# Value steps placed two units earlier, with the ones and the rows of maxima behind them, and a shorter pause in the preparation

## What is computed

```python
x = x + xcond(_layernorm(x), ctx, ctx, itok)     # attention, per batch
#   heads of 32 rows; attn = softmax(SCALE * log(itok) * q^T k) over 512 keys
#   out[d, q] = sum over k of attn[q, k] * v[d, k]
x = x + ffn(_layernorm(x), ...)
#   8 experts, top 2 of 8, capacity int(T * 1.25 / 8); gelu(x w1 + b1) w2 + b2 + gelu(x wd) wu
#   and 0.2 times a shared expert of the same form on every token
```

## Time and profile before

| | |
|---|---|
| runs | 1389.69 us (1389.59 to 1391.52) |
| profiled execution, span | 1389.7 us |
| TensorE busy | 1344.6 us (97%) |
| VectorE busy | 815.9 us (59%) |
| ScalarE busy | 686.5 us (49%) |
| GpSimd busy | 250.6 us (18%) |
| shares of the chain that ended last | PE 84%, DVE 6%, ACT 5%, issue 3% |

### The profile page before, as it was taken

The page is one execution under the profiler, slowest core; times in us unless marked ns, Lnnn a source line. Parts: engine busy times, 40 slices in busy tenths (PEclk is TensorE's granted clock), DMA queues, the critical chain, the costliest instruction groups (busy, mean ns, idle before and its releaser), DMA issues.

```text
span 1389.7 us, 27089 instructions
## 1 busy us (share of the span) xinstructions
PE 1344.6 (97%) x11195; PEld 965.9 (70%) x11213; DVE 815.9 (59%) x1337; ACT 686.5 (49%) x1024; POOL 250.6 (18%) x219
## 2 busy tenths in 40 slices
PE   5788999999999999999999999999999999999997
PEld 2152736464555646484888889998888888888895
DVE  7776768696887877763734626446264362552620
ACT  4766666757575766663423425334253342442421
POOL 4630010010010041523102204022030030300202
PEclk9799999999999999999999999999999999999999
DMA  9513131313123232408545566555564565544403
GB/s 276 182 53 107 47 99 39 107 46 99 47 84 71 69 69 92 122 17 192 167 116 152 129 131 181 131 153 135 131 166 121 133 181 127 153 119 104 98 4 39
DMA packets 136747, 155.89 MB, mean 112 GB/s; under 512 B 59065, under 2 KB 79689, under 8 KB 136626
## 3 DMA queue, kind: packets, MB, share of 16 engines
q1 hardware_dynamic: 124338, 128.97, 32.2%
q0 software_dynamic: 12288, 25.21, 10.3%
HBM read 109.47 MB, written 34.15 MB: 103 GB/s over the span
## 4 chain that ended last, share of the span: by engine, by line
PE 84%; DVE 6%; ACT 5%; issue 3%; POOL 1%; DMA 0%; POOLq 0%; ACTq 0%; DVEq 0%
PE banks L1781 25%; PE banks L1811 24%; PE banks L1697 10%; PE banks L1715 9%; PE banks L1637 3%; PE banks L1617 3%; PE banks L1585 3%; DVE rowmax L1249 2%; ACT hidden L1038 2%; DVE late_stage L1270 1%; PE banks L1833 1%; ACT QS L1025 1%; PE banks L1646 1%; PE banks L1671 1%; PE banks L1822 1%
## 5 line engine op out<-in xcount | busy, mean ns | idle before, releaser
L1811 PE MATMUL banks<-hidden,w2h 128*128 128x0 bf16 x2048 | 313.0, 273 | 0.0
L1038 ACT ACTIVATE hidden<-banks,scales 128x512 f32<-128x512 f32 x256 | 170.1, 686 | 105.7 <-PE banks L1617 82.5
L1811 PEld LDWEIGHTS banks<-hidden,w2h 128*128 128x128 bf16 x2048 | 198.5, 98 | 25.6
L1811 PE MATMUL banks<-hidden,w2l 128*128 128x0 bf16 x1024 | 195.6, 273 | 0.0
L1249 DVE TENSOR_REDUCE rowmax<-banks 128x1 f32<-128x512 f32 x256 | 172.4, 684 | 36.8 <-PE banks L1585 34.7
L1132 ACT ACTIVATE hf<-banks,b1cols 128x640 f32<-128x640 f32 x128 | 101.5, 793 | 178.9 <-PE banks L1781 173.6
L1400 DVE TENSOR_TENSOR w1l<-stage,w1h 128x2048 bf16<-128x2048 f32 x32 | 73.2, 2291 | 198.8 <-ACT w1h L1115 198.8
L1715 PE MATMUL banks<-w2h,hidden 128*128 128x512 bf16 x512 | 184.4, 379 | 0.0
L1139 ACT ACTIVATE yT<-banks 128x640 f32<-128x640 f32 (+1 forms) x32 | 22.1, 690 | 270.1 <-PE banks L1811 270.1
L1781 PE MATMUL banks<-eth,w1h 128*128 128x0 bf16 x1024 | 136.0, 276 | 0.0
L1781 PE MATMUL banks<-eth,w1l 128*128 128x0 bf16 x1024 | 135.9, 276 | 0.0
(11 more groups left out here) (193 smaller groups left out, 1971.6 us busy)
## 6 DMA issues: line engine op xcount, KB each, us to landing
stage<-in_L_ffn_w SPq DMA_DIRECT2D x64, 1024.0 KB
split_parts<-hidden SPq DMA_DIRECT2D x16, 512.0 KB, 5.6
QS<-split_parts SPq DMA_DIRECT2D x48, 128.0 KB, 2.6
KS<-split_parts SPq DMA_DIRECT2D x48, 128.0 KB, 3.1
xin<-in_x SPq DMA_DIRECT2D x16, 256.0 KB, 3.6
cin<-in_ctx SPq DMA_DIRECT2D x16, 256.0 KB, 3.2
out_rows<-xin SPq DMA_DIRECT2D x16, 256.0 KB, 2.0
normed_rows<-x2r SPq DMA_DIRECT2D x16, 256.0 KB, 2.7
```

What stands on the lines that cost most here:

```text
L1038: ac.activation(prob[n % NPH], bank(score_bank[unit]), ACT.Exp, scale=scales[:, g // 2:g // 2 + 1]).then_inc(s_exp, 1)
L1811: issued = mm(half_of(bank(b0 + j)).shape_from_register(bank_cols(e, j)), w[:, fb, rows], half_of(a[:, fb, :], j).shape_from_register(slot ...
```

## The change

Three things, all in the plan. In the exponentials the value steps 0 to 2 of a group stand in the middle of iterations 5, 9 and 13, before the side streams and `down`, instead of at the end of 6, 10 and 14. The last value step of the even group stands in iteration 3 of the odd one with the ones directly behind it; in the up pass both stand behind the third turn. The rows of maxima of the odd group start at iteration 13 instead of 12 (windows 1 to 7), right behind value step 2. And `prepare` pauses two turns instead of four behind `rstd` in windows 1 to 6, for the side stream that runs beside the even group's exponentials.

```diff
-    def prepare(g):
-        for name, gaps in (("stats", 1), ("aggr", 1), ("rstd", 4), ("norm", 1), ("x_hi", 2), ("x_lo", 1), ("c_lo", 1), ("bounce", 1)):
+    def prepare(g, pause=4):
+        for name, gaps in (("stats", 1), ("aggr", 1), ("rstd", pause), ("norm", 1), ("x_hi", 2), ("x_lo", 1), ("c_lo", 1), ("bounce", 1)):
...
-                    side.append(prepare(g + 3 if w else g + 2))
+                    side.append(prepare(g + 3, 2) if w else prepare(g + 2))
...
+                if i % GH == 1 and i > GH:
+                    value_step(g, i // GH - 1)
+                if k == 1 and i == ONES:
+                    value_step(g - 1, QT - 1)
+                    if g - 1 in SUMMED:
+                        add("ones", g - 1)
                 if k == 0:
                     if i == (LATE + 2 if w else UNITS - 3):
                         add("parts", g + 1)
-                    elif i > (LATE + 3 if w else UNITS - 3):
+                    elif i > (LATE + 4 if w else UNITS - 3):
                         next(rows, None)
...
                 one_of(downs, 2 if k == 0 and i < 2 else 1)
-                if i % GH == 2 and (i > GH or k == 1):
-                    value_step(*divmod(g * QT + i // GH - 1, QT))
-                if k == 1 and i == ONES and g - 1 in SUMMED:
-                    add("ones", g - 1)
...
-            if n == 1:
+            if n == ONES - 1:
                 value_step(b, QT - 1)
-            if n == ONES - 1 and b in SUMMED:
-                add("ones", b)
+                if b in SUMMED:
+                    add("ones", b)
```

## The result

The changed kernel takes 1398.71 us (median of five, 1395.02 to 1400.47) against 1389.69 us before (1388.26 to 1391.52): ratio 1.0056, 95% interval 1.0039 to 1.0074. It is slower by 9.0 us where 6.0 were forecast. The profiled execution has a span of 1398.7 us and a time of 1400.47 us, the highest of its five: a time is 1.8 us more than the span of the same execution. The span of the kernel before, 1389.7, likewise belongs to the highest of its runs (1391.52), so the two traces differ by 9.0 as the medians do.

What follows compares the result with a forecast made beforehand. TensorE bounds the kernel, busy 73.16 of a steady window's 73.79 us. 1389.7 + 8.5 (windows 1 to 7) - 2.5 (window 0) = 1395.7 us; forecast 1392.5 to 1399.5, 8-in-10 range 1387 to 1401.5.

Steps and rivals of the forecast that it cites:

- Joins, 3.1 us for the ones: On TensorE, all 13 blocks of ones move directly behind a value step, each join saving 0.24 us.
- the 1.1 for window 1: Window 1 was to be 1.1 us longer: unit 2 late by 1.6, partly taken back by an idle stretch.
- Rows join, 1.4 us: On TensorE, rows of maxima joined to a value step save 0.20 us in each of 7 odd groups.
- VectorE's list 1.1 late behind step 0: Step 0 ahead of score 12 makes VectorE's list, its sum and ScalarE's exponential 10 come 1.1 us later.
- The pause, "moved, and not for nothing": On ScalarE, copies of x and context now precede exponential 11, so TensorE's unit 13 stalls about 0.5 us.
- `y` late, four copies, unit 2 late by 1.6: ScalarE's y 1.0 us later, then four row copies instead of three; odd group's unit 2 1.6 late, window 1.1 longer.
- Windows 5 and 6, 1.6 each: Small routing operations in VectorE's list make each of these windows lose 1.6 us.
- Window 7, 0.9: Without copies or normalization, but with four routing operations a unit, window 7 loses 0.9 us.
- Window 0, gain 2.5, between 0 and 4: In window 0, step 2 moves into TensorE's idle time before the rows of maxima, gaining 2.5 us.
- the joins winning: Rival: ScalarE and VectorE have more slack or the copies fit; 1382.7 us, down to 1378.5; chance 0.15.
- the cancellation: Rival: loss per window half the forecast's, y in time, unit 13 not waiting; 1390.7 us; chance 0.18.
- The clock did not fall in windows 2 to 7: Rival: stalls drop the clock to 1.2 GHz there, some 1.5 us each; 1404.7 us; chance 0.12.

Runs made afterwards that it cites:

- x4: Kernel before the change with only the last value step and the ones joined: 1388.83 us (one run), steady window 73.30 us against 73.79.
- x7: x6 with the pause cut from four turns to two: 1385.15 us (one run), steady window 73.28 us.
- x8: x7 with the parts of the normalised rows and the rows of maxima one iteration earlier in windows 1 to 6: 1385.14 us (five runs), ratio 0.9964.
- x2: Changed kernel with the rows of maxima back at iteration 12, not joined to value step 2: 1391.38 us (one run), steady window 74.06 us.
- x11: x6 with value step 2 alone one score earlier in windows 1 to 7: 1389.36 us (one run), steady window 73.80 us.
- x12: x6 with the rows of maxima one unit later in windows 1 to 7: 1385.42 us (one run), steady window 73.80 us.
- x9: x6 with value step 0 alone one score earlier in windows 1 to 7: 1390.61 us (one run), steady window 73.57 us.
- x3: Changed kernel with value step 0 of the even groups back behind unit 6 in windows 1 to 7: 1390.15 us (one run), steady window 74.37 us.
- x10: x6 with value step 1 alone one score earlier in windows 1 to 7: 1382.70 us (one run), steady window 73.32 us.
- x1: Changed kernel with the old pause of four turns: 1388.83 us (one run), steady window 74.43 us.
- x6: x4 with value steps 0 to 2 early in window 0 alone: 1384.80 us (five runs), ratio 0.9963 to the kernel before.
- x5: Kernel before the change with only value steps 0 to 2 one score earlier: 1393.05 us (one run), steady window 74.52 us.

## Why the prediction came out as it did

The direction, the range and the mechanism held; the size was 3.0 us short (1395.7 against 1398.71). The text took the span 1389.7 and the median 1389.69 for one and the same. They are not: the span belongs to the run of 1391.52. The span and the median after happen to agree in the same way (1398.7 and 1398.71), so the 3.0 is the same by either; that is luck.

- *Joins, 3.1 us for the ones:* right for a steady window. x4 has 0.49 there, two joins of 0.24. The Trainium skill ("TensorEngine Tiling (Array Packing)", "Key Properties") states that a change of the tiling mode drains the engine. The trace agrees, and the 0.24 is what one join was worth here. In window 1 it is a loss instead: the step there runs at half clock, and the ones directly behind it now do so too. The changed kernel, beside the earlier trace rows:

```profile
124.41 1.16 PE L1619 MATMUL banks<-QS,KS 128*128 128x512 bf16 x2 [1.64 <-ACT hidden L1040]
125.50 1.93 PE L1639 MATMUL banks<-hidden,VT 128*32 128x512 f32 x8
127.21 1.93 PE L1648 MATMUL banks<-late_stage,ones_f 128*32 128x512 f32 x8
```

  Two blocks of 1.93. In the kernel before only the step was at this speed, and the ones, apart from it, took 1.26 at 129.33. x4 alone makes window 1 longer by 0.59 (72.06 against 71.47). The ones do not always stay slow: they last 1.46 and 1.55 in x7 and x8 (window 1 at 71.58 and 71.65), 1.28 in x2 and 1.23 in x11. The term that was mis-sized is the 1.1 for window 1: +1.8 was measured. The text had the step at half clock before it and did not ask what a block joined to it does there. The place of the rows counts too: with them at 12 again (x2) window 1 is 71.33 against 73.30, so the join need not be all of it.
- *Rows join, 1.4 us:* not visible as a gain. It is in the sum as 0.20 a window, but the later place that it needs costs 0.50 alone (x12) and 0.40 beside the early steps. The text had that cost too, as one more row copy behind `y` (0.61).
- *VectorE's list 1.1 late behind step 0:* right to 0.01 for the sum and for exponential 10. What it costs in a steady window alone was not asked: 0.27 (x9), and 0.51 inside the change (x3). The text did not have the last score of the odd group, which in x9 waits 0.25 for a late maximum.
- *Step 1 points to the same place:* it costs nothing, with the rest away (x10).
- *The pause, "moved, and not for nothing":* right inside the change, 0.45 (x1), and nothing where ScalarE keeps its gap (x7). The reason given was half of it: with the gap used up but the rows ahead of unit 13 (x2) the pause costs 0.03 by the account above. The remark that it would then also take 1 us off ScalarE's later queue found no gain: 73.28 against 73.30.
- *`y` late, four copies, unit 2 late by 1.6:* 1.5 by the timeline; `y`, and exponential 0, 0.1 earlier than forecast. Unit 13 waits 0.28 by its note, 0.5 forecast. The window came out as 1.09 for 1.1.
- *Windows 5 and 6, 1.6 each:* 1.7 and 1.5. *Window 7, 0.9:* 1.6, mis-sized by 0.7. Step 0 alone makes this part 1.4 longer (42.18 from its start to the `wdh` matmuls in x9 against 40.80 in x6), five times its cost in a steady window.
- *Window 0, gain 2.5, between 0 and 4:* 3.5 in the trace, 4.6 by the mean of the later traces, some 2.8 by the medians. Step 2 stands in the idle time, at full clock, and the rows wait 0.33 instead of 2.26:

```profile
44.59 1.06 PE L1639 MATMUL banks<-hidden,ones_f 128*32 128x512 f32 x8
45.47 1.04 PE L1639 MATMUL banks<-hidden,VT 128*32 128x512 f32 x8
...
47.16 0.41 PE L1601 MATMUL banks<-identb,MS 128*32 128x128 bf16 x16 [0.33 <-DVE MS L1260]
```

- *Behind window 7:* the sum had no term for it. The trace has 1.8 + 0.8 there; the 1.8 goes with the fall of the clock in the last pass, which other kernels have or do not have whatever their plan. With it away, the forecast would have been some 1.2 short, so part of the miss is the luck of that execution.
- *The rivals:* the joins winning is shut out by the waits at units 13 and 2, and so is the cancellation, which had unit 13 without one. The clock did not fall in windows 2 to 7: value steps last 1.06 behind the 0.99 of idle time. It fell behind 1.64 in window 1 and behind 1.00 in the last pass, and elsewhere behind less: x8 has 1.09, 0.95 and 0.95 in window 1 and a value step of 1.94 behind them. So the argument that a wait of 1.0 is shorter than one of 1.56 did not carry; that the clock stayed up in windows 2 to 7 is what the traces show, and why is open.

Added up against the trace: window 1 (+0.7), window 7 (+0.7) and the part behind it (+2.6) were too low by 4.0, and window 0 gained 1.0 more than forecast. That is 3.0, and the span is 1398.7 - 1395.7 = 3.0 above the forecast.

## What to carry to other kernels

Two edits that look like one (blocks next to each other, blocks earlier) are worth pricing apart. Joining the last value step and its ones paid 0.24 a join in the steady windows. A block moved ahead of a matmul that an in-order engine was waiting for cost 0.27 (step 0) and 0.50 (step 2), and nothing where another wait ended later (step 1). A wait in the middle of a full in-order queue may be set by the amount of work between two fixed points: reordering moved it from 0.55 to 0.31, and the trace shows ScalarE nearly full there, but less work was not tried. An edit that is free in one schedule (x7) can cost 0.45 us in another, here with the gap used up by an early step 0 and the rows no longer in TensorE's wait.

## What the runs showed of the hardware

A value step of 8 records is 1.06 us at the full clock and 1.93 at half clock, and ones joined to a slow step can be slow with it (1.93 in the changed kernel's window 1, 1.26 before). The clock does not go by the longest idle stretch alone. It fell behind 1.00 us with 0.40 and 0.29 shortly ahead of it (the last pass of the changed kernel) and stayed up behind 0.99 with 0.45 and 0.29 ahead of it (x5, the same place). It fell in x9 behind five notes of at most 0.52, and stayed up behind the same notes in x10 and x11. And the same window 0 ends up to 3.5 us earlier or later from one trace to another (its next window starts at 96.53 to 100.02 in the eleven kernels with that plan), while the steady windows of one trace agree to 0.02 us: a change of 0.1 us a window can be read in one trace, though it is far inside the spread of the times.
